# A six-layer decoder block on one core: the last attention and the last expert stage in two lanes of two rows each, and all copies of transposed weights on ScalarE

## The reference

```python
x = x + _L0_xattn_ref(ctx, ctx, _layernorm(x), ...)   # A
x = x + _L0_attn_ref(_layernorm(x), ...)              # B
x = x + _L0_ffn_ref(_layernorm(x), ...)               # C: 8 experts, top 2
x = x + _L1_xattn_ref(_layernorm(x), ctx, ctx, ...)   # D: attention to the last keys
x = x + _L1_attn_ref(_layernorm(x), ...)              # E
x = x + _L1_ffn_ref(_layernorm(x), router_w, w1, w2)  # F
```

```python
top_w, top_i = jax.lax.top_k(softmax(xf @ router_w.T), 2)
h = jax.nn.gelu(einsum('nc,ech->enh', xf, w1), approximate=False)   # 512 inner features
out = einsum('ne,enc->nc', comb, einsum('enh,ehc->enc', h, w2))
```

## Time and profile before

| | us |
|---|---|
| median of 3 runs | 322.12 (321.19 to 323.83) |
| the profiled execution, its own time | 322.6 |
| its span, first to last instruction | 320.5 |
| PE busy in the span | 252.0 (79%) |
| DVE busy | 183.8 (57%) |
| ACT busy | 121.5 (38%) |
| POOL busy | 40.5 (13%) |

### The profile page before, as it was taken

The page is one execution under the profiler, slowest core; times in us unless marked ns, Lnnn a source line. Parts: engine busy times, 40 slices in busy tenths (PEclk is TensorE's granted clock), DMA queues, the critical chain, the costliest instruction groups (busy, mean ns, idle before and its releaser), DMA issues.

```text
span 320.5 us, 4776 instructions
## 1 busy us (share of the span) xinstructions
PE 252.0 (79%) x1860; PEld 166.8 (52%) x1860; DVE 183.8 (57%) x488; ACT 121.5 (38%) x251; POOL 40.5 (13%) x48
## 2 busy tenths in 40 slices
PE   8889668767759888699995786861048899999995
PEld 8346446546424574234672555730045656767775
DVE  6573688867446769998644566747944452111112
ACT  1443669733260105333207767104033163333220
POOL 4000000000200018266210000115003010000000
PEclk9975999977795999999999999967559999999999
DMA  7950000002960120000000000000000000000000
GB/s 230 304 191 0 3 1 2 2 2 66 429 292 0 49 85 2 0 0 0 0 2 2 2 0 2 4 0 1 0 0 0 2 1 0 3 0 0 2 0 33
DMA packets 5387, 13.73 MB, mean 43 GB/s; under 512 B 2161, under 2 KB 3313, under 8 KB 4722
## 3 DMA queue, kind: packets, MB, share of 16 engines
q1 hardware_dynamic: 4064, 10.73, 9.2%
q10 hardware_dynamic: 1298, 2.66, 2.6%
HBM read 13.13 MB, written 0.26 MB: 42 GB/s over the span
## 4 chain that ended last, share of the span: by engine, by line
PE 34%; DVE 11%; ACT 6%; POOL 2%; issue 1%; DVEq 0%; POOLq 0%
PE BK L1803 12%; PE BK L1816 9%; ACT WTF L787 4%; PE BK L1980 2%; PE BK L1993 2%; PE BK L1845 2%; POOL RSTD L568 2%; PE BK L1894 1%; PE BK L1904 1%; DVE STAT L867 1%; PE BK L1997 1%; DVE MX L1331 1%; PE BK L1503 1%; DVE XH L891 1%; PE BK L1889 1%
## 5 line engine op out<-in xcount | busy, mean ns | idle before, releaser
L1803 PE MATMUL BK<-XT,WTF 128*128 128x512 f32 x128 | 58.2, 596 | 0.9 <-DVE WTF L1280 0.8
L1803 PEld LDWEIGHTS BK<-XT,WTF 128*128 128x128 f32 x128 | 23.4, 190 | 27.2 <-issue 23.5
L568 POOL TENSOR_TENSOR RSTD<-VE,MHALF 128x2 f32<-128x2 f32 x14 | 9.6, 702 | 194.7 <-DVE VE L882 153.4
L1297 DVE SCALAR_TENSOR_TENSOR X<-BK,CW,X 128x128 f32<-128x128 f32 x32 | 9.0, 344 | 43.8 <-PE BK L1816 43.8
L1816 PEld LDWEIGHTS BK<-WTF 128*128 128x128 f32 x256 | 29.7, 192 | 3.3 <-issue 3.3
L1816 PE MATMUL BK<-WTF 128*128 128x128 f32 x256 | 29.7, 275 | 0.0
L773 ACT ACTIVATE WTF<-BK 128x512 f32<-128x512 f32 x32 | 18.8, 597 | 28.8 <-PE BK L1803 28.8
L707 ACT ACTIVATE WTF<-BK 128x512 f32<-128x512 f32 x40 | 22.5, 601 | 7.8 <-PE BK L1605 7.7
L1063 DVE TENSOR_SCALAR WTF<-WTF 128x512 f32<-128x512 f32 x40 | 16.8, 422 | 12.2 <-ACT WTF L707 11.8
L1515 PE MATMUL BK<-ident 128*128 128x128 f32 x160 | 21.4, 295 | 0.3 <-DVE SM L1039 0.3
L1515 PEld LDWEIGHTS BK<-ident 128*128 128x128 f32 x160 | 20.6, 211 | 0.9 <-DVE SM L1039 0.6
(11 more groups left out here) (257 smaller groups left out, 420.9 us busy)
## 6 DMA issues: line engine op xcount, KB each, us to landing
WTF<-w_f_dram SPq DMA_DIRECT2D x2, 2048.0 KB, 15.0
WTF<-w_c_dram SPq DMA_DIRECT2D x1, 2048.0 KB, 7.8
decay<-c_decay_dram ACTq DMA_DIRECT2D x1, 1024.0 KB, 7.2
decay<-mask_q_dram SPq DMA_DIRECT2D x1, 1024.0 KB, 4.9
crows_sb<-c_rows_dram ACTq DMA_DIRECT2D x1, 544.0 KB, 8.0
w_e_sb<-w_e_dram SPq DMA_DIRECT2D x1, 480.0 KB, 3.8
w_b_sb<-w_b_dram SPq DMA_DIRECT2D x1, 384.0 KB, 4.8
WTF<-win_dram SPq DMA_DIRECT2D x1, 320.0 KB, 4.2
```

What stands on the lines that cost most here:

```text
L568: pool.tensor_tensor(RSTD[:, pair], VE[:, pair], MHALF[:, pair], ALU.pow).then_inc(ln_rstd, 1)
L1803: ins = pe.matmul(hbank(u), w1[:, o:o + P], XT[:, :], start=True, stop=True)
```

## The change

**Stages E and F** become one stage with two lanes. Lane 0 is rows 0 and 1, lane 1 is rows 2 and 3. Each step of E and F is a function of the lane h with 256 columns in place of 512, on four PSUM banks of its own (lane 0: 0 to 3, lane 1: 4 to 7). On each engine the steps of the two lanes are put in a row by hand: lane 0 goes through E first, and lane 1's steps from the rotation on are put between lane 0's steps and between lane 0's experts; lane 1's experts come last. `up` has two banks for each lane, where it had six. Each lane's result has a DMA of its own.

**The functions on ACT**: `silu(x)` is written as x (1 + tanh(x/2)) / 2. ACT makes `Tanh`, which is in one table with `Exp`; the copy of x is a further instruction of ACT (q, g) or read from PSUM; DVE makes the product (`gated_xT`, `gated_q`, `gate_out`, `gated_ff`), and the halves are put into constants. The router's `Exp` of two logits becomes one `Tanh` of half their difference.

**Stage D**: ACT makes the copies of all four groups; DVE makes none.

```diff
...
-                        for g in (0, 2):
+                        for g in range(4):
...
-                            act.activation(PT[:, b % 2, 4 * g:4 * g + 4, :], bank(4), ACT.Copy).then_inc(d_pT, 1)
+                            act.activation(PT[:, b % 2, 4 * g:4 * g + 4, :], bank(4 + g % 2), ACT.Copy).then_inc(d_pT, 1)
...
+                    def rotate(h):
+                        pair = lane_pair(h)
+                        qk, qr, q2 = flat(QK[:, pair]), flat(QR[:, pair]), flat(Q2[:, pair])
+                        pool.wait_ge(l_q, h + 1)
+                        settle(pool.tensor_tensor(qr, qk, cs[:, 0, pair], ALU.mult))
+                        for b in range(2):
+                            for f in range(2):
+                                settle(pool.tensor_tensor(halves(q2)[:, b, :, f, :], halves(qk)[:, b, :, 1 - f, :],
+                                                          halves(cs[:, 1, pair])[:, b, :, f, :], ALU.mult))
+                        pool.tensor_tensor(qr, qr, q2, ALU.add).then_inc(l_rot, 1)
...
+                    lane_power(LN_E, 0)
+                    lane_power(LN_E, 1)
+                    rotate(0)
+                    rotate(1)
...
+                    def gate_xT(h):
+                        act.wait_ge(l_hc, h + 1)
+                        act.activation(XT[:, lane_cols(h)], HT[:, lane_cols(h)], ACT.Tanh).then_inc(l_th, 1)
...
+                        act.activation(LGT[:, :, pair, :].rearrange("p r b h -> p b r h"),
+                                       qkvg[:, :, WE_R:WE_G].rearrange("p b (r h) -> p b r h", r=2), ACT.Copy).then_inc(l_qkv, 1)
+                        act.activation(QK[:, pair].rearrange("p b a n -> p b (a n)"), qkvg[:, :, 0:128], ACT.Copy).then_inc(l_qkv, 1)
+                        act.activation(TQ[:, pair, :], qkvg[:, :, 0:64], ACT.Tanh, scale=0.5).then_inc(l_qkv, 1)
+                        act.activation(VV[:, pair, :], qkvg[:, :, 128:256], ACT.Copy).then_inc(l_qkv, 1)
+                        act.activation(GS[:, pair, :], qkvg[:, :, WE_G:WE_O], ACT.Copy).then_inc(l_qkv, 1)
+                        act.activation(TG[:, pair, :], qkvg[:, :, WE_G:WE_O], ACT.Tanh, scale=0.5).then_inc(l_qkv, 1)
...
+                    def deviation(h):
+                        act.wait_ge(l_vs, h + 1)
+                        act.activation(SM2[:, lane_pair(h), :], SM1[:, lane_pair(h), :], ACT.Sqrt, bias=col("eps4"), scale=4.0 / HD)\
+                           .then_inc(std_ready, 1)
...
+                    def gate_ff(h, js=range(3)):
+                        for j in js:
+                            w = FFT[j][1]
+                            act.wait_ge(l_ff_ps, 3 * h + j + 1)
+                            act.activation(HF[0:w, j, lane_cols(h)], lane_bank(h, (2, 3, 0)[j])[0:w, 0:256], ACT.Tanh, scale=0.5)\
+                               .then_inc(l_ffs, 1)
...
+                    def gelu(h, e):
+                        if e >= 2:
+                            act.wait_ge(e_y_ps, NE * h + e - 1)
+                        for p in range(2):
+                            act.wait_ge(e_h_ps, before_f + 2 * NE * h + 2 * e + p + 1)
+                            act.activation(GT[:, e % 2, 2 * p:2 * p + 2, lane_cols(h)],
+                                           lane_bank(h, 2 + p).rearrange("p (a n) -> p a n", a=2), ACT.Gelu).then_inc(e_act, 1)
...
+                    take_qkvg(0)
+                    between(0)
+                    take_qkvg(1)
+                    square(0)
+                    deviation(0)
+                    context(0)
+                    between(1)
+                    second_xT(0)
+                    gate_ff(0)
+                    last_xT(0)
+                    route(0)
+                    gelu(0, 0)
+                    gelu(0, 1)
+                    square(1)
+                    gelu(0, 2)
+                    deviation(1)
+                    gelu(0, 3)
+                    context(1)
+                    gelu(0, 4)
+                    second_xT(1)
+                    gelu(0, 5)
+                    gate_ff(1)
+                    gelu(0, 6)
+                    last_xT(1)
+                    gelu(0, 7)
+                    route(1)
+                    for e in range(NE):
+                        gelu(1, e)
 
...
+                    def gated_xT(h):
+                        dve.wait_ge(l_th, h + 1)
+                        half = XT[:, lane_cols(h)]
+                        dve.scalar_tensor_tensor(out=half, in0=half, scalar=1.0, in1=HT[:, lane_cols(h)],
+                                                 op0=ALU.add, op1=ALU.mult).then_inc(l_xt, 1)
...
+                    first_stats(0)
+                    first_stats(1)
+                    lane_norm(LN_E, 0, X)
+                    lane_norm(LN_E, 1, X)
+                    convolve(0)
+                    gated_xT(0)
+                    convolve(1)
+                    gated_xT(1)
+                    choices(0)
+                    gated_q(0)
+                    gate_out(0)
+                    shares(0)
+                    weights(0)
+                    outputs(0)
+                    centred(0)
+                    bypass(0)
+                    variances(0)
+                    gated_q(1)
+                    contexts(0)
+                    choices(1)
+                    attended(0)
+                    shares(1)
+                    lane_norm(LN_E2, 0, CT)
+                    gate_out(1)
+                    weights(1)
+                    gated_ff(0)
+                    finished(0)
+                    lane_norm(LN_F, 0, X)
+                    outputs(1)
+                    chances(0)
+                    centred(1)
+                    best_two(0)
+                    bypass(1)
+                    variances(1)
+                    weigh(0, 0)
+                    contexts(1)
+                    weigh(0, 1)
+                    weigh(0, 2)
+                    attended(1)
+                    lane_norm(LN_E2, 1, CT)
+                    weigh(0, 3)
+                    gated_ff(1)
+                    weigh(0, 4)
+                    finished(1)
+                    lane_norm(LN_F, 1, X)
+                    weigh(0, 5)
+                    chances(1)
+                    weigh(0, 6)
+                    weigh(0, 7)
+                    best_two(1)
+                    for e in range(NE):
+                        weigh(1, e)
 
 
...
+                    def up(h, e):
+                        for p in range(2):
+                            if e:
+                                pe.wait_ge(e_act, before_f + 2 * NE * h + 2 * e + p - 1)
+                            for i in range(2):
+                                o = (4 * e + 2 * p + i) * P
+                                ins = pe.matmul(lane_bank(h, 2 + p)[:, 256 * i:256 * i + 256], w_f1[:, o:o + P], XT[:, lane_cols(h)],
+                                                start=True, stop=True)
+                            ins.then_inc(e_h_ps, 1)
...
+                    def down(h, e):
+                        if e == 0:
+                            pe.wait_ge(r_z, 2 + h)
+                        if e >= 2:
+                            pe.wait_ge(e_sum, NE * h + e - 1)
...
+                    lane_norm_T(LN_E, 0, 0)
+                    lane_norm_T(LN_E, 1, 0)
...
+                    project_qkvg(0)
+                    project_qkvg(1)
+                    turn_context(0)
+                    project_context(0)
                     stay_warm(3)
-                    norm_T(LN_E2, 5)
-                    pe.wait_ge(ln_xT, xT_count(LN_E2))
-                    for j, (o, w) in enumerate(FFT):
-                        for c in range(2):
-                            bk = j if c == 0 else (3, 4, 6)[j]
-                            o2 = WE_FF + FF * c + o
-                            pe.matmul(BK[0:w, bk, :], w_e[:, o2:o2 + w], XT[:, :], start=True, stop=True).then_inc(l_ff_ps, 1)
-                    pe.wait_ge(l_ff, 3)
-                    for b in range(B):
-                        for j, (o, w) in enumerate(FFT):
-                            ins = pe.matmul(BK[:, (7, 5)[b // 2], b * P:(b + 1) * P], HF[0:w, j, b * P:(b + 1) * P],
-                                            w_e2[0:w, j, :], start=(j == 0), stop=(j == 2))
-                        if b % 2:
-                            ins.then_inc(proj_ps, 1)
+                    lane_norm_T(LN_E2, 0, 1)
+                    ff_up(0)
+                    ff_down(0)
+                    stay_warm(3)
+                    lane_norm_T(LN_F, 0, 0)
+                    logits(0)
+                    pe.wait_ge(loads["w_f1"], 16)
+                    pe.wait_ge(loads["w_f2"], 16)
+                    up(0, 0)
+                    up(0, 1)
+                    down(0, 0)
+                    up(0, 2)
+                    down(0, 1)
+                    up(0, 3)
+                    turn_context(1)
+                    down(0, 2)
+                    project_context(1)
```

(14 more changed lines are left out.)

746 lines of the change are left out of this document (410 added, 336 removed).

## The result

The changed kernel took 316.19 us (median of 4 executions, 312.26 to 319.86) against 322.31 us beside it (4 executions, 321.19 to 323.83). The ratio is 0.9713, with a 95% interval of 0.9629 to 0.9797; it compares only executions in which the granted clock was not disturbed. Two later sets of 6 gave medians of 314.46 and 313.63 us, the first of them with a ratio of 0.9766 (0.9725 to 0.9807). All 16 executions have a median of 313.9 us, the 33 of the kernel before in this study 322.5. So the change saves about 8.6 us, 2.7%; by the two ratios it is 9.3 and 7.5 us. The forecast was 3.9 us, at 318.2.

What follows compares the result with a forecast made beforehand. PE alone was taken to bound stage F, and a serial chain over DVE, ACT and POOL much of E. Terms summed to -4.5 us, -3.9 with hand-overs, so 322.1 became 318.2 us; range 314.8 to 322.4.

Steps and rivals of the forecast that it cites:

- Stage D, +0.4: All weight copies on ACT: at most 0.17 us more for each of three rows; +0.4 taken, bounds -0.3 and +4.0.
- E until the context, -2.9 - 0.3 - 4.9 = -8.1: Lane 0 at half width: projection -2.9 us, choice and rotation -0.3, products to context -4.9.
- Context to F's start, -3.6: Lane 0's context to first `up`: three pieces, -5.4 us at full clock, -3.6 with one of two clock falls.
- Leg 1: Lane 0's context to second norm's transposes: 8.9 us, +1.4, because POOL stretches `choices(1)`, which stands ahead of `attended(0)`.
- the fall of the clock in leg 2 or 3: Half clock in the inner network gives back 1.9 us, slow warming ahead of F 1.7; one of the two taken.
- Legs 2 and 3: Second norm's transposes to inner `down`'s end, then to first `up`: 6.3 and 4.2 us at full clock, -5.2 and -1.6.
- Stage F, +5.9 + 0.3 + 1.3 - 0.5 - 0.2 = +6.8: Experts: lane 1's matmuls +5.9 us, 64 more matmuls +0.3, second expert's `up` stall +1.3, last weighing -0.5, last DMA -0.2.
- 0.6 for rounded hand-overs: Lane 0's 30 or so operations between engines cost 0.02 us more each, taking the sum from -4.5 to -3.9.
- The cover of lane 1 that I called thin: Lane 1's E under lane 0's experts: results come 0.3 to 0.5 us before PE asks at three places.
- clock stays up: Rival, chance 0.15: warmed PE keeps 2.4 GHz from lane 0's context to F; 317.0 us, 316 with nothing rounded up.
- ACT and DVE hold lane 0's experts: Rival, chance 0.11: in stage F, in-order lists wait behind lane 1's work and PE idles; 326.6 us, slower.
- the collisions: DVE operations stretched by POOL's lane 1 work; the range's lower end takes off another 1.2 us for their not coming.

Runs made afterwards that it cites:

- the second and third profiles: The changed kernel run twice more with nothing edited, one profile each; medians 314.46 and 313.63 us (6 executions each).
- the first profile: The changed kernel's first profiled execution, nothing edited: span 312.2 us, own time 314.05 us.
- wide_rot: The changed kernel with `rotate(1)` over all four rows again, so POOL's instructions are as wide as before; median 313.20 us (4).
- choices_late: The changed kernel with `choices(1)` moved behind `attended(0)` on DVE; median 314.03 us (4).
- less_warm: The changed kernel with 2 in place of 13 warming matmuls ahead of lane 0's second-norm and last-norm transposes; median 315.00 us (4).

## Why the prediction was wrong

The sign and the structure were right, the size was not: 3.9 forecast, about 9.0 by the stretches and 8.6 by the medians. Step by step, against the second and third profiles (the misses add up: 0.4 + 0.7 + 3.8 + 0.6 - 0.4 = 5.1):

- *Stage D, +0.4*: measured 0.0 to 0.1.
- *E until the context, -2.9 - 0.3 - 4.9 = -8.1*: measured 15.34 in place of 24.11 = -8.8, with the projection at half clock in both. In the first profile, where it ran at full clock, -10.2. From the products to the context I had 6.5 us; in the first profile it was 219.32 to 225.82, 6.5. Choice and rotation took 5.7 us there (213.65 to 219.32) where I had 6.5: POOL's four 64-column products took 1.67 us together, 0.42 each, not 0.6.
- *Context to F's start, -3.6*: measured 17.2 in place of 24.6 = -7.4. **This is the step that failed**, by 3.8 of the 5.1 us. Two things were in it. Leg 1 was priced at 8.9 us because `choices(1)` would be stretched by POOL, end some 2.4 us late and hold `attended(0)` behind PE's projection; the leg took 5.9 to 6.3. The choices took 1.8 us and were done before PE was, `attended(0)` waited for PE and not for them, and even POOL instructions as wide as before cost them only 1.0 more (wide_rot). I had taken one row, L1440 at 1.30 us beside a 512-column sum, and let nine operations meet all of POOL's 4.2 us. The kernel before has three more such rows, of 1.26, 0.69 and 0.56 us:

```profile
218.83 1.26 DVE L1431 TENSOR_TENSOR SCR<-SCR 128x32 f32<-128x32 f32 x1
...
220.38 0.69 DVE L1433 COPY SCR<-SCR 128x16 f32<-128x16 f32 x1
...
221.47 0.56 DVE L1439 TENSOR_TENSOR SM<-SCR 128x64 f32<-128x64 f32 x1
```

  Each of the four ended 0.03 to 0.08 us after the POOL instruction during which it had started. In these rows an operation thus loses at most the rest of one POOL instruction. In the changed kernel four of POOL's six take 0.35 to 0.43 us, and three of the nine choices (two reductions, a reciprocal) are of a kind that no row shows held up: some 0.2 us was lost, against the 1.66 us that the nine took with no such POOL work beside them (choices_late).

  The other thing is the fall of the clock in leg 2 or 3, 1.8: it did not come in any of the three profiles, because the 26 records of warming stand directly ahead of each leg (less_warm brings it about by taking them out). Legs 2 and 3 at full clock took 11.3 us where I had 6.3 + 4.2 = 10.5, which goes 0.8 the other way.
- *Stage F, +5.9 + 0.3 + 1.3 - 0.5 - 0.2 = +6.8*: measured +7.2. The stall ahead of the second `up` is 1.87 us, the 1.9 that I had named for a start at 248 and not the 1.3 that I took.
- *0.6 for rounded hand-overs*: nothing of it is seen. The terms taken from rows already held them.

The cover of lane 1 that I called thin held everywhere: no wait of PE above 0.3 us for it in lane 0's experts. Of the rivals, *clock stays up* came nearest, with 317.0; what it lacked most was leg 1, shorter by 2.6 to 3.0 us. *ACT and DVE hold lane 0's experts* did not occur; each of the two loads with a square root fell into ACT's slack. The range ended at 314.8 because its lower end kept half of the collisions in. What I said the profile would show was right for the place of the stall, the gapless F and D's period; wrong for the first `up` (243.4 to 246.2, not 248 to 251), for `attended(0)`, which waits 0.78 us for PE and not for the choices, and for the clock, which was at 1.00 through legs 2 and 3. Lane 1's matmuls filled 5.6 us of F, near the 5.9.

Table loads again took 1.28 us with the next function right behind (load of `Sqrt` at 223.22, the function at 224.52). The drain of about 1.38 us that the Trainium skill adds (ScalarE: Activation LUTs, "What ACT_TABLE_LOAD costs") is not in this trace either; with it the stall, which has one load in it, would be 3.2 us, an estimate by that page's figure, and it is 1.87.

## What to carry to other kernels

Where one half of a batch leaves PE idle between short pieces and a later stage is all PE, interleaving the other half's serial chain into that stage can be worth most of that chain (20.8 us here, some 4 of them clock, of 28.7 that it took in series), while the same two lanes without that cover were slower than the four rows together. Price an interference from which instructions start while the other engine's is running, and for how long that one still runs, not from the worst row. And where the clock moves whole times by 5 us in stages nobody edited, compare stretches between fixed instructions at the same clock; a gain of 1.9 us was plain in them and invisible in six whole executions.
